# The exact search for doubtful rows as a loop over heads and rounds on one scratch row

## The reference

```
qn, kn = q / norm(q), k / norm(k)
scores = einsum('bhqd,bhkd->bhqk', qn, kn) / temp
kk = S // 4                              # 64 of 256
vals, idx = top_k(scores, kk)            # per row
w = softmax(vals)                        # all others get weight 0
out = w (scattered to its places) @ v
```

## Time and profile before

| what | value |
|---|---|
| median of three runs | 3950.44 us |
| the profiled execution's own time | 3949.0 us |
| its span | 3947.1 us |
| TensorE's mean granted clock | 0.884 of full speed |
| PE, DVE, ACT, POOL busy | 76%, 71%, 54%, 48% |
| branches at L1648 | 128 |
| first of the eight largest at L1640 | 136 |

### The profile page before, as it was taken

One profiled execution on the slowest core, in us unless ns is written; L12 is line 12 of the kernel. 1 busy time (PEld: TensorE's weight loads), 2 busy tenths in 40 slices (PEclk: granted clock), 3 DMA queues, 4 the chain that ended last, 5 costly groups with the idle time before them and its releaser, 6 DMA issues. The chain is left out here.

```text
span 3947.1 us, 59251 instructions
## 1 busy us (share of the span) xinstructions
PE 3015.7 (76%) x16154; PEld 1684.0 (43%) x16154; DVE 2799.5 (71%) x9325; ACT 2132.2 (54%) x5970; POOL 1875.5 (48%) x2307
## 2 busy tenths in 40 slices
PE   3687888887788778778877888888877887778855
PEld 2244444444444444444444444444443444444432
DVE  4467768776777777777777776877777777677772
ACT  1455555565555565555655555566555565555541
POOL 0345555453465444455444555454445544445423
PEclk7888899998889988889988889998898998889877
DMA  5000000000000000000000000000000000000000
GB/s 179 6 15 20 7 21 21 15 21 20 18 10 20 15 20 21 20 7 20 20 15 20 21 12 16 20 15 21 20 21 7 20 21 15 20 17 15 10 9 11
DMA packets 43387, 80.95 MB, mean 21 GB/s; under 512 B 3692, under 2 KB 11884, under 8 KB 42758
## 3 DMA queue, kind: packets, MB, share of 16 engines
q1 hardware_dynamic: 41254, 68.75, 5.1%
q0 software_dynamic: 1504, 5.77, 0.4%
HBM read 57.73 MB, written 16.78 MB: 19 GB/s over the span
## 5 line engine op out<-in xcount | busy, mean ns | idle before, releaser
L476 POOL TENSOR_SCALAR probs<-probs,kept_inv 128x256 f32<-128x256 f32 x1024 | 639.3, 642 | 1231.6 <-DVE kept_inv L1661 1231.6
L1632 DVE SCALAR_TENSOR_TENSOR probs<-scores,threshold,probs 128x256 f32<-128x256 f32 x1007 | 451.6, 505 | 369.6 <-issue 369.2
L741 ACT ACTIVATE near<-scores 128x256 f32<-128x256 f32 x1024 | 413.9, 428 | 160.0 <-DVE nearest L1602 160.0
L721 ACT ACTIVATE scores<-score_ps,neg_guess 128x256 f32<-128x256 f32 x1024 | 398.9, 492 | 146.2 <-DVE kept_inv L1661 87.0
L1598 DVE MATCH_REPLACE8 near<-nearest,near 128x256 f32<-128x256 f32 x1024 | 406.6, 406 | 0.0
L979 PE MATMUL work_ps<-ident,probs 128*128 128x128 f32 x2072 | 341.9, 308 | 53.3 <-POOL probs L476 25.2
L449 POOL TENSOR_TENSOR inv_norm<-sumsq,minus_half 128x32 f32<-128x32 f32 x64 | 373.3, 5833 | 5.3
L1594 DVE MAX8 nearest<-near 128x8 f32<-128x256 f32 x1024 | 356.8, 409 | 0.3
L1602 DVE MAX8 nearest<-near 128x8 f32<-128x256 f32 x1024 | 356.8, 409 | 0.0
L756 ACT ACTIVATE probsT<-work_ps 128x512 f32<-128x512 f32 x512 | 291.6, 599 | 106.3 <-PE work_ps L1144 75.1
L1675 DVE SCALAR_TENSOR_TENSOR rows<-gate_t,rows 128x512 f32<-128x512 f32 x64 | 51.8, 810 | 404.3 <-POOL rows L497 404.3
(11 more groups left out here) (167 smaller groups left out, 5756.8 us busy)
## 6 DMA issues: line engine op xcount, KB each, us to landing
x_in<-in_x_dram SPq DMA_DIRECT2D x32, 512.0 KB, 3.5
x_res<-in_x_dram SPq DMA_DIRECT2D x32, 512.0 KB, 4.4
out_dram<-rows SPq DMA_DIRECT2D x32, 512.0 KB, 3.0
c_sb<-in_ctx_dram SPq DMA_DIRECT2D x32, 256.0 KB, 2.8
scores<-in_L_ffn_W_dram SPq DMA_DIRECT2D x4, 1024.0 KB, 5.3
near<-in_L_ffn_W_dram SPq DMA_DIRECT2D x4, 1024.0 KB, 5.3
w_q<-in_L_attn_Wq_dram POOLq DMA_DIRECT2D x1, 1024.0 KB, 10.7
probs<-in_L_xattn_Wq_dram SPq DMA_DIRECT2D x1, 1024.0 KB, 9.9
```

The costliest lines, as they stand in the source:

```text
L476: pool.tensor_scalar(probs[:, s % 2, h, j], probs[:, s % 2, h, j], kept_inv[:, s % 2, n:n + 1], 1.0, ALU.mult, ALU.mult).then_inc(s_pr, 1)
L721: last = act.activation(scores[:, s % 2, h, j], score_ps[:, j, h], ACT.Identity, bias=neg_guess[:, t, n:n + 1])
L741: last = act.activation(near[:, h, j], scores[:, s % 2, h, j], ACT.Sign, accum_out=sign_sum[:, s % 2, n:n + 1])
L1632: step.mark(dve.scalar_tensor_tensor(out=probs[:, r, h, j], in0=scores[:, r, h, j], scalar=threshold[:, r, k:k + 1], in1=probs[:, r, h, j] ...
```

## The change

The exact side of keep_top is no longer written out for each head. It is a loop over the eight heads, whose register indexes the buffers; inside it, for a head with doubtful rows, the 256 scores are copied to a scratch row, a second loop does the eight rounds on that row, and the masking reads it. Each head and each round ends with a wait for its own last instruction and a clear of s_slow. After the loop one instruction adds 8 to s_dve, as the eight marks did. The scratch row is made of the memory of picked and same, which become two halves of one tensor; top8 needs only one set of eight. The side without doubtful rows is the same eight instructions.

```diff
-        picked = sb("picked", [P, HS, WINDOW])
-        same = sb("same", [P, HS, WINDOW])
+        trials = sb("trials", [P, 2, HS, WINDOW])
+        picked, same = trials[:, 0], trials[:, 1]
+        row = trials[:].rearrange("p a h n -> p (a h n)")
...
-        top8 = sb("top8", [P, HS, 8])
+        top8 = sb("top8", [P, 8])
...
@@ -1626,37 +1627,45 @@
                 dve.sem_inc(s_seq_v, 1)
                 n = dve.value_load(unsure_n[0:1, r, HS:HS + 1].bitcast(I32), min_val=0, max_val=MOST)
                 before = step.n
-
-                def keep_above(k):
-                    h, j = divmod(k, HQ)
-                    step.mark(dve.scalar_tensor_tensor(
-                        out=probs[:, r, h, j], in0=scores[:, r, h, j], scalar=threshold[:, r, k:k + 1],
-                        in1=probs[:, r, h, j], op0=ALU.is_ge, op1=ALU.mult, accum_out=kept_sum[:, r, k:k + 1]))
-
-                def keep_struck(k):
-
-                    h, j = divmod(k, HQ)
-                    for n in range(ROUNDS):
-                        slow.wait(slow.mark(dve.max(top8[:, k], scores[:, r, h, j])))
-                        slow.wait(slow.mark(dve.match_replace(scores[:, r, h, j], top8[:, k], scores[:, r, h, j],
-                                                              STRUCK)))
+                rows_s = scores[:, r].rearrange("p a h k -> p (a h) k")
+                rows_p = probs[:, r].rearrange("p a h k -> p (a h) k")
+
+                def one(view, k):
+                    return view[:, bass.ds(k, 1)].rearrange("p u k -> p (u k)")
+
+                def strike():
+                    slow.wait(slow.mark(dve.max(top8[:], row)))
+                    slow.mark(dve.match_replace(row, top8[:], row, STRUCK))
                     slow.restart()
-                    step.mark(dve.scalar_tensor_tensor(
-                        out=probs[:, r, h, j], in0=scores[:, r, h, j], scalar=STRUCK / 2,
-                        in1=probs[:, r, h, j], op0=ALU.is_le, op1=ALU.mult, accum_out=kept_sum[:, r, k:k + 1]))
 
                 with dve.If(n > 0):
-                    for k in range(HS):
-                        n_k = dve.value_load(unsure_n[0:1, r, k:k + 1].bitcast(I32), min_val=0, max_val=MOST)
+                    with dve.Fori(0, HS) as k:
+                        n_k = dve.value_load(unsure_n[0:1, r, bass.ds(k, 1)].bitcast(I32), min_val=0, max_val=MOST)
                         with dve.If(n_k > 0):
-                            keep_struck(k)
+                            slow.mark(dve.tensor_copy(row, one(rows_s, k)))
+                            slow.restart()
+                            with dve.Fori(0, ROUNDS):
+                                strike()
+                            slow.mark(dve.scalar_tensor_tensor(
+                                out=one(rows_p, k), in0=row, scalar=STRUCK / 2, in1=one(rows_p, k),
+                                op0=ALU.is_le, op1=ALU.mult, accum_out=kept_sum[:, r, bass.ds(k, 1)]))
+                            slow.restart()
                         with dve.Else():
-                            step.n = before + k
-                            keep_above(k)
+                            slow.mark(dve.scalar_tensor_tensor(
+                                out=one(rows_p, k), in0=one(rows_s, k), scalar=threshold[:, r, bass.ds(k, 1)],
+                                in1=one(rows_p, k), op0=ALU.is_ge, op1=ALU.mult,
+                                accum_out=kept_sum[:, r, bass.ds(k, 1)]))
+                            slow.restart()
+                    dve.sem_inc(s_dve, HS)
                 with dve.Else():
                     step.n = before
-                    for k in range(HS):
-                        keep_above(k)
+                    for h in range(NH):
+                        for j in range(HQ):
+                            k = h * HQ + j
+                            step.mark(dve.scalar_tensor_tensor(
+                                out=probs[:, r, h, j], in0=scores[:, r, h, j], scalar=threshold[:, r, k:k + 1],
+                                in1=probs[:, r, h, j], op0=ALU.is_ge, op1=ALU.mult,
+                                accum_out=kept_sum[:, r, k:k + 1]))
                 step.wait(step.n)
                 dve.reciprocal(kept_inv[:, r], kept_sum[:, r]).then_inc(s_inv, 1)
```

More of the change, by code:

```diff
@@ L1609, in set_threshold @@
                 dve.wait_ge(s_se, at(b, NS * NH, NH * s + NH))
-                step.wait(step.mark(dve.tensor_tensor(picked[:], hit[:], nearest[:], ALU.mult)))
-                step.wait(step.mark(dve.tensor_reduce(cut[:], picked[:], AX.X, ALU.add)))
-                k = step.mark(dve.tensor_tensor(same[:], nearest[:],
+                step.wait(step.mark(dve.tensor_tensor(picked, hit[:], nearest[:], ALU.mult)))
+                step.wait(step.mark(dve.tensor_reduce(cut[:], picked, AX.X, ALU.add)))
+                k = step.mark(dve.tensor_tensor(same, nearest[:],
                                                 cut[:].unsqueeze(2).to_broadcast([P, HS, WINDOW]), ALU.is_equal))
@@ L1616, in set_threshold @@
                 step.wait(k)
-                step.wait(step.mark(dve.tensor_reduce(n_same[:], same[:], AX.X, ALU.add)))
+                step.wait(step.mark(dve.tensor_reduce(n_same[:], same, AX.X, ALU.add)))
                 dve.tensor_scalar(unsure[:, r], n_same[:], 1.0, None, ALU.not_equal).then_inc(s_bad, 1)
```

## The result

The kernel after takes 4013.04 us (median of four runs, 4008.39 to 4013.30), the kernel before 3948.74 (four runs, 3946.17 to 3951.39) on the same chip: ratio 1.0159, 95% interval 1.0146 to 1.0172. It is slower, as forecast, and within the range of 3980 to 4200, but by +64.3 us where +135 was forecast. The profiled execution of after has a span of 4011.3 us. Its mean granted clock of TensorE is 0.872, that of before 0.884. The lower clock lies in the batches with an exact strip (0.838 in the mean, 0.884 before); in the quiet batches it is 0.926, 0.913 before.

A forecast was written before the change was run, and what follows sets the result against it. The prediction took DVE's order plus the tail at a batch's end as the bound. Exact strips +264 us and shorter jumps -129 gave +135 on 3950.4, so 4085 us, with a range of 3980 to 4200.

The forecast's parts named there:

- The jump: Quiet strips' branch over the exact side: 2.8 us falls to 0.16; 244 us saved on DVE, 129 reaching the end.
- strip 1: Its quiet-strip gain of 74 us arrives partly, about 1.9 of 2.6 us a strip: 53 us, bounds 22 and 72.
- strip 0: Its quiet-strip gain of 71 us is lost in the wait for strip 1's count: 0, bounds 0 and 71.
- strip 3: Its quiet-strip gain arrives whole, since the batch's tail starts from its kept sums: 76 us.
- Strip 2: Its quiet-strip gain of 22 us is lost in DVE's wait for POOL's inv_norm; bounds 0 and 22.
- The exact strips: The 16 strips entering the exact side lose overlap to the loop: 264 us more (184 to 358), nothing hiding it.
- clear head: A turn of the exact side's heads loop without doubtful rows: 2.45 us, ends 2.1 and 3.0.
- doubtful head: A turn of the exact side's heads loop with copy, eight rounds and masking: 14.9 us, ends 12.6 and 17.
- A: Rival, 12%: strip 0's and strip 2's gains reach the end, saving 244 us; exact strips add 184: 3890 us.
- B: Rival, 10%: small loops cross a fetch edge at some places, 2.7 us for each outer-loop turn there: 4195 to 4305 us.
- C: Rival, 6%: the quiet strips' jump stays dear at any length, no saving: 4214 us.
- D: Rival, 8%: cheap loop, moderate saving, both low ends (184 - 148 = +36) or part of the extra covered: 3945 to 3985 us.

The follow-up runs named there:

- the pads: Kernel after plus 240 never-executed DVE instructions ending the exact side, behind a run-time branch: strip 0 alone 4021.57 us, strip 1 4082.69, strip 3 4081.56.
- all four at once: Kernel after with 240 never-executed DVE instructions at the end of the exact side in all four strips, behind a run-time branch: 4172.25 us, ratio 1.0572.
- the pad in strip 3: Kernel after with 240 never-executed DVE instructions at the end of the exact side in strip 3 alone, behind a run-time branch: 4081.56 us, ratio 1.0340.
- both edits: Kernel after with the eight rounds written out inside the heads loop and clear heads counting on s_dve without their own wait: 3880.45 us, ratio 0.9830.

## Why the prediction was right in sign and mechanism and wrong in size

**What bounds the kernel: right.** DVE time added or taken on the exact side reached the end nearly one to one: 51.0, 72.8, 122.1 and 138.9 us of it became 46, 67, 130 and 127 us of run. (The prediction says that DVE waits long at one place only. It also waits 88 us in 52 waits for ACT's signs at L1573; they stayed as they were, and nothing hangs on it.)

**The jump: right.** 0.16 us from the branch to the masking in strips 1 and 3, as taken. Quiet idle 135.5, under the 150 named; strip 1 back at 3.9 as a wait for the count; a quiet batch at 108.49 with 108 forecast. The saving, as +196.9 less +64.3, is 133 us; 129 were forecast. By strips the pads give, after what they cost the exact side, 7 to 11 us for strip 0 (forecast 0, with a bound of 71), 60 to 68 for strip 1 (53) and 63 to 68 for strip 3 (76). The sum, 130 to 147, is more than the 125 of all four at once, in which strip 0's wait covers a part of strip 1's. Strip 2 had no pad of its own: that its 22 us were lost rests on L1556's wait for POOL, which is 21.7 us longer (62.2 from 40.5). Strip 1 was put a little too low, and strip 3 was taken whole and was not: of 2.63 us a quiet batch gains 2.0 there. A likely place of the rest is L1561's wait for PE, 24.2 us before and 55.9 after, 34.2 with the pad in strip 3 and 27.2 with it everywhere: there DVE comes to work for the batch ahead before PE has its product. No run takes that wait away. So the 129 came out near in sum, in part because these misses have opposite signs.

**The exact strips: the step that failed.** The mechanism was right, the size of the term was not: +264 us forecast for the 16 exact strips, +197 measured, though within the ends of 184 to 358. Within it the clear head, 2.45 us forecast and 2.05 measured, is two thirds. The forecast for the 16 strips is 532 us, the traces have 466. The 66 us, head by head:
- A clear head was taken as 2.45 us; the 82 pairs that follow one another are 1.93 to 2.53 apart, 2.05 in the mean. 111 x 0.40 = 44 us.
- A doubtful head was taken as 14.9; from the clear head before it to the one behind it is 15.2 to 15.5 in most strips, less one clear head 13.3. 17 x 1.6 = 27 us. A round is 1.37 in the mean, not 1.43; that is 0.5 of the 1.6, and the copy, the masking and the branches around the rounds the rest.
- Start and end of a strip were 0.4 and are 0.7: 5 us back.

The pieces of a clear head, from the records of one in batch 9 (it starts at 1206.60, the second row below, and takes 2.04 us): masking to the clear's end 0.62 (0.66 + 0.21 = 0.87 forecast), count, branch back and head of loop 0.37 (0.34 + 0.08), load to the inner branch's end 0.81 (0.83), address operations 0.24 (0.33). The largest error, 0.25, is the masking: I added its duration, a start and the gap of the earlier trace rows (0.21). As I read it, that gap already held the start: the clear begins 0.04 us after the sum's read has ended, and takes 0.054. The address came out at one operation in strips of even parity and two in odd ones, where I had counted four, one for each operand with a register:

```profile
1204.56 0.48 DVE L1654 SCALAR_TENSOR_TENSOR probs<-scores,threshold,probs  x1 [1.55 <-issue]
...
1206.60 0.48 DVE L1654 SCALAR_TENSOR_TENSOR probs<-scores,threshold,probs  x1 [1.55 <-issue]
```

(odd, strip 1, DVE's timeline; the even one is the timeline of the result, 1.93 apart), and DVE's queue over the run:

```profile
L1643 DVEq TENSOR_LOAD <-unsure_n x128: 300/306/375, 870.0 to 3884.9; - x128
L1654 DVEq FUSED_REGOPS  x159: 57/93/129, 884.2 to 3883.8; - x159
L1642 DVEq COMPARE_BRANCH  x128: 50/56/69, 883.1 to 3897.9; - x128
```

159 address operations for 111 clear heads: 48 of them have the second one of 57 ns. That the overlap is lost was foreseen; only its price was put too high.

**The rivals.** A, faster, failed although the number that it names came true: the mean extra of an exact strip is 196.9/16 = 12.3 us, below the 15.2 that it asks for. But strip 0's and strip 2's gains did not reach the end, and its sum of 184 against 244 needs both. Its two halves are seen apart: the price was near its end, the saving at mine. B fell: no two clear heads are more than 2.53 us apart and no two rounds more than 1.60, where one missed line would add 2.6. The exact side was entered at 10 of the 24 places, all eight of the loop among them. (B's sum says 2.7 us a turn and multiplies 2.6; nothing hangs on it.) C fell: the jump takes 0.16 us. D, the sum of both low ends, was nearest in price (184) but its times (3945 to 3985) end 28 us short, since it also took the saving at 148 or saw the price covered. Without the doubled gap and the surplus addresses (0.25 and 0.09) a clear head would have been put at 2.11, which takes 111 x 0.34 = 38 us off: 4047.

## What to carry to other kernels

Code that is skipped is not free: 112 skips over eight written-out blocks cost this kernel about 125 us at the end, and the cure is to make what is skipped short, by a loop inside it, without making what is run slow. In such a loop the dearest thing was a wait for the body's own last instruction at its end, 0.67 us a clear head. It takes from the queue the time to load, branch and address the next turn under the present one. The loop itself with its addresses from registers is the next, 0.51 us a clear head (1.38 with it and without the wait, 0.87 written out). So let the instruction count on a semaphore that is waited for after the loop. Count a saving strip by strip against the next wait for another engine: a gain ahead of one is mostly a longer wait, as all but 7 to 11 of strip 0's 71 us were.

## What the runs showed that I had not expected

- The version with both edits takes 3880.45 us, 1.7% less than before, and heads written out with a loop for the rounds 3883.13. The first keeps the short skip, the second a shorter one than before that is near at most places, and both keep the masking running while the queue goes on.
- A skip of some 165 to 190 instructions costs 0.1 to 0.5 us at most places and 2.7 to 3.0 at others, one of them in the loop, where it does so every time; one of some 280 takes 2.7 to 3.2 at all 112 jumps. The earlier trace rows had shown only the far and the near.
- Branches back over small bodies never waited: 128 turns of the heads and 136 rounds, in the 10 places that were entered.
- A masking with four dynamic operands takes one fused register operation of 93 ns in the median, at odd parity a second of 57 ns.
- The traffic of one of the page's two instruction queues halved: q14 has 234 packets and 1.92 MB, and had 473 and 3.87 MB before; the other, q8, kept its 156 packets and 2.56 MB. Each queue's share of the DMA engines is 0.3% or less.

```profile
q14 instruction: 234, 1.92, 0.2%
```
